# The up products of an attention block's MLP as three fp32r passes instead of one fp32 product

## The reference, cut to what matters

```python
z = sum_heads @ Wout_w.T + Wout_b
u = z + _ln(z, norm_g, norm_b)
ffn = jax.nn.gelu(u @ ffn1_w.T + ffn1_b, approximate=False)
h_out = u + (ffn @ ffn2_w.T + ffn2_b)
return h_out @ proj_w.T + proj_b
```

## Time and profile before

| | us |
|---|---|
| median of 3 executions | 1163.65 |
| lowest, highest | 1159.08, 1170.48 |
| the profiled execution | 1157.41 |
| its span, first to last instruction | 1155.7 |
| mean granted TensorE clock of the span | 0.950 |

### The profile page before, as it was taken

One profiled execution on the slowest core, in us unless ns is written; L12 is line 12 of the kernel. 1 busy time (PEld: TensorE's weight loads), 2 busy tenths in 40 slices (PEclk: granted clock), 3 DMA queues, 4 the chain that ended last, 5 costly groups with the idle time before them and its releaser, 6 DMA issues.

```text
span 1155.7 us, 16233 instructions
## 1 busy us (share of the span) xinstructions
PE 1012.9 (88%) x4744; PEld 708.9 (61%) x4744; DVE 818.6 (71%) x2327; ACT 639.3 (55%) x1265; POOL 643.6 (56%) x751
## 2 busy tenths in 40 slices
PE   6788999998979999999978989899976668989996
PEld 5335777765647667667746447777834445656663
DVE  7775886758878787888674775676744678777661
ACT  2335667765565676666543336676744345455543
POOL 4006556447998888877661026555256767663440
PEclk9899999999999999999997899999987889999998
DMA  8577767740000000000002025687710000000000
GB/s 264 193 254 250 226 213 237 255 125 24 17 12 13 14 15 12 15 5 2 1 1 67 7 71 196 214 258 225 218 50 23 24 19 28 14 24 10 10 15 23
DMA packets 63495, 105.26 MB, mean 91 GB/s; under 512 B 7888, under 2 KB 42192, under 8 KB 63376
## 3 DMA queue, kind: packets, MB, share of 16 engines
q1 hardware_dynamic: 54320, 85.60, 22.8%
q0 software_dynamic: 9088, 18.63, 5.6%
HBM read 79.29 MB, written 26.87 MB: 92 GB/s over the span
## 4 chain that ended last, share of the span: by engine, by line
PE 48%; POOL 19%; DVE 13%; issue 11%; ACT 6%; DMA 1%; another core or an unknown queue 1%; POOLq 0%; SPq 0%; ACTq 0%; DVEq 0%
PE bank L208 6%; POOL wr L678 3%; PE bank L457 3%; PE bank L455 3%; PE bank L474 3%; POOL head_rstd L1379 3%; PE bank L456 3%; PE bank L453 3%; PE bank L472 3%; PE bank L473 3%; PE bank L1193 2%; PE bank L1153 2%; PE bank L1159 2%; POOL got L678 2%; PE bank L1199 2%
## 5 line engine op out<-in xcount | busy, mean ns | idle before, releaser
L622 POOL DMA_INDIRECT spare_all<-xs,list_row x156 | 158.0, 1013 | 237.0 <-DVE list_row L786 109.8
L858 DVE TENSOR_TENSOR hid_lo<-hid,hid_hi 128x512 fp32r<-128x512 f32 (+1 forms) x184 | 112.1, 611 | 74.1 <-ACT hid L559 44.7
L558 ACT ACTIVATE hid_hi<-bank,b_up_of 128x512 fp32r<-128x512 f32 (+1 forms) x138 | 86.7, 628 | 56.0 <-PE bank L457 36.8
L559 ACT ACTIVATE hid<-bank,b_up_of 128x512 f32<-128x512 f32 (+1 forms) x184 | 113.0, 624 | 5.0 <-issue 1.7
L678 POOL DMA_INDIRECT got<-ys,y_slots x80 | 85.9, 1074 | 44.6 <-DMA ys<-spare_all 26.0
L1272 ACT ACTIVATE gate_b<-bank,head_rstd 128x128 f32<-128x128 f32 x256 | 73.1, 370 | 63.5 <-POOL head_rstd L1379 63.0
L208 PEld LDWEIGHTS bank<-ident,spare_all 128*128 128x128 f32 x476 | 61.2, 151 | 69.6 <-issue 59.2
L208 PE MATMUL bank<-ident,spare_all 128*128 128x128 f32 x476 | 78.8, 290 | 22.1 <-DVE spare_all L401 15.7
L559 ACT ACTIVATE hid<-bank,cols_sb 128x512 f32<-128x512 f32 x64 | 44.0, 687 | 91.5 <-PE bank L453 79.1
L455 PE MATMUL bank<-xh,wr 128*128 128x512 f32 (+1 forms) x184 | 78.9, 429 | 13.2 <-issue 7.0
L1379 POOL TENSOR_TENSOR head_rstd<-head_var,neg_half 128x4 f32<-128x4 f32 x64 | 75.9, 1186 | 5.3
(11 more groups left out here) (325 smaller groups left out, 2694.2 us busy)
## 6 DMA issues: line engine op xcount, KB each, us to landing
wr<-wq SPq DMA_DIRECT2D x92, 512.0 KB
wq<-wr SPq DMA_DIRECT2D x16, 512.0 KB, 5.7
ys<-spare_all SPq DMA_DIRECT2D x32, 256.0 KB
got<-in_w_mlp SPq DMA_DIRECT2D x8, 512.0 KB, 5.6
xs<-spare_all SPq DMA_DIRECT2D x16, 256.0 KB, 2.3
spare_all<-xs,list_row POOLq DMA_INDIRECT x156
out_x<-X SPq DMA_DIRECT2D x8, 256.0 KB, 2.3
ys<-in_x SPq DMA_DIRECT2D x1, 1920.0 KB
```

Of the source, the lines that this page charges most:

```text
L559: nc.scalar.activation(hid[:, n % HC, 0:w], bank[up_bank(n)][:, 0:w], ACT.Gelu_apprx_tanh, bias=bias).then_inc(s["gelu_done"], 1)
L622: g.indirect_dma_start(out=xin[:, j % XIN, b], out_offset=None, in_=xs, in_offset=bass.IndirectOffsetOnAxis(ap=list_row[:, n:n + 1], axis=0))\
L858: v.tensor_tensor(hid_lo[:, q, 0:w], hid[:, n % HC, 0:w], hid_hi[:, q, 0:w].bitcast(F32), ALU.subtract).then_inc(s["lo_done"], 1)
```

## The change

The weights `f1` and the moving operand `uT` are each split into a high part, rounded to fp32r by ScalarE, and a low part, what is left, by VectorE. The four parts lie in the first four 512-column pieces of `wr`. For all tiles but the last, an up product is three fp32r passes into one PSUM group: high weights by high u, low weights by high u, high weights by low u. The last tile (`LAST`, 7) keeps the fp32 product.

- Once: ScalarE copies `f1` to its high part in slot 3; VectorE subtracts it in slot 4; TensorE waits for that in slot 15.
- Per tile, seven times: ScalarE's `keep_u` reads bank 6 twice, first for the high part, then for `uT`; VectorE has one more subtraction (`rest_of_u`), in phase 7 between the scan and the head statistics; `up` waits for that (`u_lo_ready`) instead of for `uT_ready`.

```diff
--- before.py
+++ after.py
@@ -1084,13 +1084,17 @@
         mix_rows = hid_hi[:, 5:7]
         mix_hi = hid_hi[:, 7, 0:2 * P].rearrange("r (k e) -> r k e", e=P)
         mix_sign = hid_hi[:, 7, 2 * P:3 * P]
+        LAST = TILES - 1
+        unit = wr[:].rearrange("p r h l n -> p (r h l) n")
+        f1_parts, u_parts = [unit[:, k] for k in (0, 1)], [unit[:, k] for k in (2, 3)]
 
         def mix_sems():
             return {k: sem(f"mix_{k}") for k in (
                 "stats_ready", "rstd_ready", "xn_ready", "xn_turned", "w_hi_ready", "w_lo_ready", "rows_ready", "x_hi_ready", "x_lo_ready",
                 "dx_in", "dx_ready", "ab_in", "ab_out", "hs_ready", "c_in", "o_ready", "ot_in", "o_stats", "p_in",
                 "head_rstd", "share_ready", "added", "base_in", "base_out", "z_stats", "z_rstd", "un_ready", "u_ready", "u_in", "uT_ready",
-                "f1_in", "f1_out", "f2_in", "hT_ready", "y_in", "tile_done")}
+                "f1_in", "f1_out", "f2_in", "hT_ready", "y_in", "tile_done",
+                "u_lo_ready")}
 
 
 
@@ -1182,7 +1186,10 @@
                 turn(pe, bank[6], lambda b: u[:, b]).then_inc(s["u_in"], 1)
 
             def up(i, n):
-                pe.wait_ge(s["uT_ready"], i + 1)
+                if i < LAST:
+                    pe.wait_ge(s["u_lo_ready"], i + 1)
+                else:
+                    pe.wait_ge(s["uT_ready"], i + 1)
                 for c in (2 * n, 2 * n + 1):
                     if c == 0 and i + 2 < TILES:
                         pe.wait_ge(s["x_lo_ready"], i + 3)
@@ -1190,7 +1197,13 @@
                         pe.wait_ge(s["hT_ready"], i)
                     if c >= 2:
                         pe.wait_ge(s["f1_out"], i * HC + c - 1)
-                    nc.tensor.matmul(bank[7 - c % 2][:], f1[:, c * P:(c + 1) * P], uT[:], start=True, stop=True).then_inc(s["f1_in"], 1)
+                    out, w = bank[7 - c % 2], [blk(part, c) for part in f1_parts]
+                    if i == LAST:
+                        nc.tensor.matmul(out[:], blk(f1, c), uT[:], start=True, stop=True).then_inc(s["f1_in"], 1)
+                        continue
+                    nc.tensor.matmul(out[:], w[0], u_parts[0], start=True, stop=False)
+                    nc.tensor.matmul(out[:], w[1], u_parts[0], start=False, stop=False)
+                    nc.tensor.matmul(out[:], w[0], u_parts[1], start=False, stop=True).then_inc(s["f1_in"], 1)
 
             def down(i, n):
                 if n == 0:
@@ -1225,6 +1238,8 @@
                     down(two_before, phase - DOWN_AT[0])
                 if n == BASE:
                     pe.wait_ge(s["rows_ready"], 1)
+                if n == NH + NH - 1:
+                    pe.wait_ge(s["w_lo_ready"], 4)
                 if phase == BASE and tile is not None:
                     base(tile)
                 if phase == Y_AT and two_before is not None:
@@ -1310,6 +1325,8 @@
                 act.wait_ge(s["u_in"], i + 1)
                 if i > 0:
                     act.wait_ge(s["hT_ready"], i)
+                if i < LAST:
+                    nc.scalar.activation(u_parts[0], bank[6][:], ACT.Identity, bias=nb)
                 nc.scalar.activation(uT[:], bank[6][:], ACT.Identity, bias=nb).then_inc(s["uT_ready"], 1)
 
             def gelu(i, n):
@@ -1330,6 +1347,8 @@
                     keep_head(n)
                 if 0 <= n - 3 < HEADS:
                     share_head(n - 3)
+                if n == 3:
+                    nc.scalar.copy(f1_parts[0], f1[:]).then_inc(s["w_hi_ready"], 1)
                 if phase == 3 and n // NH + 1 < TILES:
                     mix_normalize(act, s, tile + 1)
                 if phase == UN and before_it is not None:
@@ -1481,6 +1500,10 @@
                 first = no_carry[:, 0:1] if i % 2 == 0 else carry[:, h:h + 1]
                 v.tensor_tensor_scan(hs[:, q % 2], a_sb[:, q % 2], b_sb[:, q % 2], first, ALU.mult, ALU.add).then_inc(s["hs_ready"], 1)
 
+            def rest_of_u(i):
+                dve.wait_ge(s["uT_ready"], i + 1)
+                v.tensor_tensor(u_parts[1], uT[:], u_parts[0].bitcast(F32), ALU.subtract).then_inc(s["u_lo_ready"], 1)
+
             def h_of(i):
                 dve.wait_ge(s["f2_in"], i + 1)
                 if i > 0:
@@ -1538,8 +1561,13 @@
                     carry_head(n - 1)
                 if n < HEADS:
                     scan_head(n)
+                if phase == NH - 1 and before_it not in (None, LAST):
+                    rest_of_u(before_it)
                 if 0 <= n - 2 < HEADS:
                     head_stats(n - 2)
+                if n == 4:
+                    dve.wait_ge(s["w_hi_ready"], 4)
+                    v.tensor_tensor(f1_parts[1], f1[:], f1_parts[0].bitcast(F32), ALU.subtract).then_inc(s["w_lo_ready"], 1)
                 if phase == add_at + 1 and n // NH + 1 < TILES:
                     mix_x_stats(dve, steps, s, tile + 1)
                 if phase == 3 and before_it is not None:
```

## The result

| | before | after |
|---|---|---|
| median of 20 executions each, us | 1161.64 | 1171.76 |
| lowest, highest | 1155.02, 1170.48 | 1162.06, 1177.19 |
| the profiled execution, its span | 1157.41, 1155.7 | 1173.15, 1171.4 |
| mean granted TensorE clock | 0.950 | 0.952 |

The ratio after to before is 1.0075, 95% interval 1.0051 to 1.0098: the change costs 0.75%, 8.7 us (the difference of the two means; the medians lie 10.1 apart), where +4.2 us (0.36%) were forecast. The sign, the class (within 1%) and the range held; the size of the whole did not.

What follows compares the result with a forecast made beforehand. The bound was the chain of waits over L0's attention: POOL at both ends, a 41.5 us round per tile between. Tiles 3.4, tile 6 0.28 and split 0.5 gave +4.2 us: 1163.65 to 1167.9 us, range 1158 to 1176.

Steps and rivals of the forecast that it cites:

- The stall: Tiles 0 to 5, phase 7: TensorE idles 1.01 to 1.71 us before the first up pass, awaiting u's low part.
- The second pair: Second pair of up products in each tile: no new wait, gives back another 0.33 us.
- Tile 6's stall: End of L0's heads: 1.08 us stall, of which 0.28 us come through to POOL after slack.
- The saving of 0.66 a tile: Up products of tiles 0 to 5: six passes take 1.39 us per pair for 1.72, 3.96 us in all.
- I take 0.5 us; the ends are 0 and 0.7: One-time split, slot 4: VectorE's subtraction of f1 holds up POOL's fetch at 287.51, costing 0.5 us.
- the first collision: Slot 4: POOL's fetch meets the split's subtraction and ends at 289.12 in place of 288.62.
- A stall of 1.1 us should leave it there: Tile 1: TensorE's granted clock, 1.00 despite a 1.81 us idle gap, stays there under the new stall.
- The low part in time: Rival, phase 7: VectorE subtracts before TensorE arrives, leaving only the saving; 1160.2 us, not slower; 15%.
- POOL held in every tile: Rival, tiles 0 to 3: subtraction delays POOL's fetch 0.61 us each, 2.4 on top, 1170.3 us; 20%.
- both operations on the ring: Rival, tile cycle: VectorE's 0.69 and ScalarE's 0.57 no longer hide, 1.68 us per tile, 1175.4 us and more; 10%.

Runs made afterwards that it cites:

- the run with fp32 products: Kernel after with all up products fp32, the wait for the low part of u kept: 1139.99 us, ratio 1.0083 to the kernel before.
- the reordered one: Kernel after with VectorE's low-part subtraction put ahead of o and the scan in phase 7: 1130.18 us, ratio 0.9984 to the kernel before.
- the run without the wait: Kernel after with all up products fp32 and waiting only for uT, added work kept: 1133.51 us, ratio 1.0016 to the kernel before.
- the run with the split early alone: Kernel after with only ScalarE's f1 copy moved to slot 1 and VectorE's subtraction to slot 3: 1171.2 us, ratio 1.0044 to the kernel before.

## Why the prediction was right or wrong

**The mechanism held.** The stall stands where it was put, behind the scan in VectorE's list, seven times, and the first pass starts 1.96 us after the start of the scan in tile 0. The passes come 0.23 us apart. The second pair waits for nothing and tiles 0 to 5 add 3.44 us where 3.4 were forecast, tile by tile within 0.22. Tile 6's stall came through to L395 with 0.28, as forecast. The runs show the cause by both signs: the stall goes with the place of the subtraction (-0.73 a tile), and grows with a second one (+0.6 a tile). The saving of 0.66 a tile was 0.68 against the run with fp32 products, and 0.72 where no stall is left.

**"I take 0.5 us; the ends are 0 and 0.7": this term of the sum was mis-sized.** The split cost 1.17 us, beyond its upper end. I priced the first collision alone (0.37 us measured), and took what POOL does next as unchanged. A late POOL made its next root start 0.27 us into a scan instead of 0.10 ahead of it, and lost 0.80 more. Moved by a slot, the split costs nothing. **A term was missing:** the gap at head 60, 0.34, which no row of the kernel before has. With both the sum is 3.4 + 0.28 + 1.17 + 0.34 = 5.19; measured were +5.25 and +5.30 over the stretch. That the whole kernel's time lay in the range says less: the range is 18 us wide, and of the 8.7 us measured 3.5 don't lie in the stretch that the sum is about.

**The clock.** "A stall of 1.1 us should leave it there" was right for the kernel after in its two profiles, without a fall in the tiles. But the reason given, that it held through the gap of 1.81 us ahead of u's transposes, was a reading of one execution, and the earlier trace rows begin 2.3 us behind the gap's end. The kernel before lost it behind just that gap in another.

**The rivals.** The low part in time fell in this kernel, and is just what the reordered one does: 329.75 in the stretch. POOL held in every tile and both operations on the ring fell with the run without the wait and the table by heads. The collision behind the first of them is real, but costs time in single tiles only. In both profiles of the kernel after, the scans of two slots (24 and 40) take 2.41 us beside POOL's addition, which they don't before, and the shift is back two slots later.

**What stays open.** Ratio and stretch differ by some 3.5 us in the first measurement (8.7 against 5.25), and on the second chip by -1.6 (3.7 against 5.3). The part from L395 to the routing took 35.4 and 35.6 us in the kernel before, 37.7 in the kernel after both times and in three more runs, but 32.7 to 32.9 in four, with fp32 products and with passes. TensorE's granted clock over it differs with them: 0.71 in the kernel before, 0.64 in the kernel after, 0.75 to 0.79 in the four. Whether the change moves this part isn't settled: the sum of the two parts fits the ratios no better than the stretch alone. That the longer idle times make falls of the clock more frequent over many executions is possible too, and no run here shows it.

## What to carry to other kernels

When an operation is added on one engine and another waits for it, its price is the list that stands ahead of it, the scan here, more than its own length; look for the place in the list where the consumer still has work, and put it there. Here that turned +5.3 into -3.5 us of the stretch with the same instructions, 1.0 of it by chance. Splitting a product into cheaper passes pays only what the records show (1.39 for 1.72 us), and an operation moved against GpSimd has to be followed one collision further than the first.

## What the runs showed of the hardware

**A scan and GpSimd lengthen each other.** The scan, usually 1.27 us, took 2.70 in the kernel before:

```profile
329.63 2.70 DVE L1482 TENSOR_TENSOR_SCAN spare_all<-spare_all,carry 128x512 f32<-128x512 f32 x1
```

with POOL's addition of two SBUF tiles starting 0.32 us behind it:

```profile
329.95 1.30 POOL L1388 TENSOR_TENSOR pick<-pick,gate_b 128x512 f32<-128x512 f32 x1
```

The addition keeps its 1.30 here, and the scan pays. In slot 4 of the kernel after it is POOL's root that pays (1.85). The same pair can cost either engine: at 389.01 in the kernel before, the addition starts 0.28 us behind the scan's start, and it is the addition that takes 2.07, the scan its 1.28. And it can cost neither: the root at 311.05 above. The start times in a trace don't tell beforehand which it will be, though the 2.70 of this scan stands in all twelve profiles. The Trainium skill, in "SBUF — State Buffer", section "SBUF: two separate sides", says that whichever starts first holds the shared ports for the whole instruction. The root's 1.85, the subtraction's 1.69 and 1.75 agree. The scan of 329.63 doesn't: by the trace it starts ahead of the addition and is the one that gets longer. Nor does the root at 311.05. Whether a start in the trace lies ahead of the first access, no run here tells.

**TensorE's clock fell after the same gap in some executions and not in others.** Ahead of u's transposes in tile 0 it was idle for 1.81 us in both profiles of the kernel before. The windows behind it, the first profile and the second:

```profile
337.00:340.00 3.00, 2.32 (x11) 1.74 (x12) 3.00 (x7) 3.00 (x9) 2.77 (x3) 1.00 0.06 18
```

```profile
336.00:339.00 3.00, 2.65 (x9) 2.26 (x10) 2.93 (x7) 2.46 (x7) 2.77 (x3) 0.58 0.08 22
```

The granted clock stayed at 2.4 GHz once (1.00), and fell to the 1.2 GHz level once, for some 3 us. The fall came with a loss of 1.07 us there, and of 2.49 in the run with the split early alone, where the late subtraction then met POOL's addition. A difference of that size between two single profiles is no effect of a change until the granted clock of the stretch has been read in both.
